# Self attention of a four-layer decoder: queries and keys turned once per entry and fetched per group from a DRAM scratch

## The reference, cut to what matters

```python
for l in range(N_LAYERS):
    h = rmsnorm(x, n1[l])
    q, k, v = jnp.split(h @ Wqkv[l].T + bqkv[l], 3, axis=-1)
    q = apply_rope(split_heads(q, H), cos, sin)      # H = 16, 8 features a head
    k = apply_rope(split_heads(k, H), cos, sin)
    o = merge_heads(sdpa(q, k, v, causal_bias)) @ Wo[l].T + bo[l]
    x = x + o
    ...                                               # cross attention, feed forward
```

## Time and profile before

| | us |
|---|---|
| three runs | 2101.96, 2107.96, 2116.95 |
| median | 2107.96 |
| span of the profiled execution | 2100.9 |
| median less that span | 7.1 |
| self attention of layer 1, first to last tile of maxima | about 1026 to 1210 |

### The profile page before, as it was taken

The page is one execution under the profiler, slowest core; times in us unless marked ns, Lnnn a source line. Parts: engine busy times, 40 slices in busy tenths (PEclk is TensorE's granted clock), DMA queues, the critical chain, the costliest instruction groups (busy, mean ns, idle before and its releaser), DMA issues. The chain is left out here.

```text
span 2100.9 us, 34690 instructions
## 1 busy us (share of the span) xinstructions
PE 1827.5 (87%) x13011; PEld 1120.1 (53%) x13011; DVE 1415.5 (67%) x3427; ACT 1067.7 (51%) x1523; POOL 784.6 (37%) x1131
## 2 busy tenths in 40 slices
PE   5978998594777898899999999999999989989978
PEld 4557664373544444564544565644555554456557
DVE  8667776543676877864577885567786467787475
ACT  2655655131453566564466566366656446656510
POOL 4423324403624453431455342245443155443130
PEclk9999999597787898998999999999999999999989
DMA  7443333121000000141000033000014000003200
GB/s 227 111 137 101 109 104 97 63 69 39 21 1 13 1 1 13 37 110 43 16 1 1 1 93 84 28 1 1 1 44 120 14 16 2 1 26 99 52 1 21
DMA packets 69995, 100.91 MB, mean 48 GB/s; under 512 B 17126, under 2 KB 35438, under 8 KB 69188
## 3 DMA queue, kind: packets, MB, share of 16 engines
q1 hardware_dynamic: 60612, 90.01, 14.9%
q0 software_dynamic: 9216, 8.69, 1.6%
HBM read 52.43 MB, written 12.38 MB: 31 GB/s over the span
## 5 line engine op out<-in xcount | busy, mean ns | idle before, releaser
L1806 DVE TENSOR_REDUCE maxima<-wide 128x2 f32<-128x512 f32 (+3 forms) x512 | 406.1, 819 | 134.2 <-PE wide L836 130.7
L2042 ACT ACTIVATE prob<-wide 128x768 f32<-128x768 f32 (+1 forms) x384 | 332.2, 881 | 149.7 <-PE wide L836 149.4
L1965 ACT ACTIVATE prob<-wide 77x1024 f32<-77x1024 f32 x256 | 257.8, 1017 | 89.8 <-PE wide L836 86.5
L836 PE MATMUL wide<-q_g 32*128 32x256 f32 (+3 forms) x2048 | 268.5, 394 | 37.5 <-ACT prob L2042 18.1
L2284 POOL TENSOR_SCALAR_AFFINE_SELECT prob<-prob 128x256 f32<-128x256 f32 (+1 forms) x384 | 184.9, 487 | 296.4 <-ACT prob L2042 294.6
L1482 DVE TENSOR_REDUCE maxima<-wide 128x8 f32<-128x616 f32 x256 | 202.9, 795 | 110.7 <-PE wide L836 106.7
L836 PEld LDWEIGHTS wide<-q_g 32*128 32x128 f32 x2048 | 140.0, 188 | 205.6 <-issue 100.1
L2106 POOL TENSOR_TENSOR rstd<-moments,cst 128x4 f32<-128x4 f32 x88 | 90.4, 1027 | 360.7 <-DVE moments L1370 173.8
L1886 ACT ACTIVATE q_g<-wide 128x1024 fp32r<-128x1024 f32 x128 | 131.1, 1024 | 179.3 <-PE wide L836 177.4
L1886 ACT ACTIVATE q_g<-acc 128x512 fp32r<-128x512 f32 x192 | 114.5, 596 | 144.0 <-PE acc L836 139.0
L2191 POOL DMA_DIRECT2D masked_k<-kx x224 | 121.2, 546 | 177.4 <-PE wide L836 176.3
(11 more groups left out here) (253 smaller groups left out, 3096.1 us busy)
## 6 DMA issues: line engine op xcount, KB each, us to landing
masked_q<-q_g SPq DMA_DIRECT2D x448, 64.0 KB
masked_q<-mask_l SPq DMA_DIRECT2D x84, 308.0 KB
masked_k<-kx POOLq DMA_DIRECT2D x224, 19.5 KB, 1.9
A<-in_w SPq DMA_DIRECT2D x2, 2048.0 KB, 12.2
unit_w<-in_unit_w SPq DMA_DIRECT2D x8, 448.0 KB, 3.9
ffn_w<-in_ffn_w SPq DMA_DIRECT2D x4, 768.0 KB, 4.7
slots_in<-v_third SPq DMA_DIRECT2D x1, 2560.0 KB, 12.6
prob<-slots_in SPq DMA_DIRECT2D x8, 320.0 KB, 3.1
```

What stands on the lines that cost most here:

```text
L836: return e.matmul(out, lhsT, rhs, start=start, stop=stop, is_transpose=turn)
L1806: e.tensor_reduce(top[:, t, h], v[:, :, at0:at0 + P * t + P], AX.X, ALU.max, negate=True).then_inc(*made("max", *([("free", tile)] if t == ...
L1965: e.activation(p[0:SC, :], s[0:SC, :], ACT.Exp, bias=0.0, scale=1.0).then_inc(*made("exp", pb, ("free", tile)))
L2042: e.activation(pv, sv, ACT.Exp, bias=0.0, scale=8 ** -0.5).then_inc(*made("exp", pb, ("free", tile)))
```

## The change

Queries and keys of an entry are rotated as before (with columns reordered so that a partition after the turn is a feature of a head in a group, and the tables widened to 32 columns and loaded by a DMA of their own, `rope`). `qk_turn` now runs once per entry: eight turns of 128 x 128, one ACT copy back into `qkv`. `qk_cut` takes the high part in one DVE instruction of 128 x 1024 and the low part in one POOL subtraction of 128 x 1024. `qk_store` writes them with three DMAs of 512 KB each into a DRAM scratch (ring of three, 2 MB each) in the row order of the heads; `qk_fetch` brings 128 x 1024 (512 KB) per group into `q_g`. Rows with ones lie in the scratch from three start-up DMAs. After the maxima, DVE writes 32 columns into a small tile, `self_full` is one turn of those 32 columns, ACT copies 32 x 128, and `self_max` lays eight rows of 512 into `q_g` by an SP DMA. In the order, `spread` (turn, cut, store) sits in the prepare of g = 3 at rows 1, 4 and 9, the fetch at row 4 of prepare (13 for the first), and the attend and finish rows are shifted: two logits tiles in attend (rows 8, 10), four in finish (rows 0, 2, 4, 6), where there were four and two. `o_turn` and `out_turn` move to a fifth phase.

```diff
@@ self_steps
+    def spread(b, *rows):
+        return in_rows(*zip(rows, (("qk_turn", l, b), ("qk_cut", l, b), ("qk_store", l, b))))
     def prepare(b, g):
         if (l, b, g) == (0, 0, 0):
-            return in_rows((11, ("qk_turn", l, b, g)))
+            return in_rows((13, ("qk_fetch", l, b, g)))
...
-        phase, c = in_rows((8, ("qk_turn", l, b, g))), b + 1
-        if b and g == 0:
-            phase = beside(in_rows((2, ("cut_k", l, b))), phase)
         if c < B:
             phase = beside(phase, *[[normalise(c)],
                                     [project_in(c), rotate(c, (0, 10))],
-                                    [rotate(c, (1, 1), (2, 3), (3, 6), (4, 8))],
-                                    [rotate(c, (5, 1)), in_rows((4, ("cut_q", l, c)))]][g])
+                                    [rotate(c, (1, 1), (2, 3), (3, 6), (4, 8), (5, 11))],
+                                    [spread(c, 1, 4, 9)]][g])
...
     def attend(b, g):
-        return in_rows((1, ("self_full", l, b, g)), (4, logits(0, 2)), (6, logits(0, 0)), (8, logits(1, 2)),
-                       (10, logits(1, 0)), (12, ("self_values", l, b, g, 0)))
+        return in_rows((1, ("self_full", l, b, g)), (2, ("self_max", l, b, g)), (8, logits(0, 2)), (10, logits(0, 0)))
     def finish(b, g):
-        s = [(0, logits(2)), (2, logits(0)), (4, values(1)), (8, values(2)), (10, values(3))]
+        s = [(0, logits(1, 2)), (2, logits(1, 0)), (4, values(0)), (4, logits(2, 2)), (6, logits(2, 0)), (8, values(1)),
+             (12, values(2)), (12, values(3))]
...
-    turned = beside(rotate(0, *[(k, k // 2) for k in range(6)]), in_rows((3, ("cut_q", l, 0)), (3, ("cut_k", l, 0))),
+    turned = beside(rotate(0, *[(k, k // 2) for k in range(6)]), spread(0, 3, 3, 4),
@@ sync
+            for dram in qk_rows:
+                e.dma_start(dram[:, :].rearrange("(i r x) c -> i r x c", i=HG, x=4)[:, :, 3, :],
+                            io["qk_rows"].unsqueeze(0).broadcast_to([HG, PART, G * 2 * S]))
+            def qk_store(l, b):
+                to = qk_rows[at][:, :].rearrange("(m x) c -> m x c", x=4)
+                for w in need(("sq_top", l, b), ("sq_cut", l, b), T.freed("qk_rows", held)):
+                    e.wait_ge(*w)
+                e.dma_start(to[:, 0, :], t[:, 1:3, :])
+                e.dma_start(to[:, 1, :], t[:, 1::2, :])
+                e.dma_start(to[:, 2, :], t[:, 0::2, :])
+            def qk_fetch(l, b, g):
+                for w in need(("qk_stored", l, b), ("qk_rows",), T.freed("q_g", held)):
+                    e.wait_ge(*w)
+                e.dma_start(q_g[at], of[:, 2 * S * g:2 * S * g + 2 * S])
+            def self_max(l, b, g):
+                for w in need(("mx_turned", l, b, g)):
+                    e.wait_ge(*w)
+                e.dma_start(qk[SELF_MAX:P:SELF_STEP, 0, :].bitcast(F32), mx_t[at].bitcast(F32))
@@ tensor
+                for k in range(2):
+                    for t in range(NI):
+                        i_mm = mm(s[:, S * k + P * t:S * k + P * t + P], src[:, t, k, :], ident, turn=True)
...
-                turn_queries(a, cut_queries(("sqt", l, b)), g)
+                mm(a[0:2 * HG * NI, 0:P], maxima_in[g % 2][:, :, :, :].rearrange("p i k t -> p (i k t)"), ident, turn=True)
```

More of the change, by code:

```diff
@@ L293, in quantised @@
                  [("qkv", 0, b, 0)], [("qkv", 0, b, 1), ("bias_o", 0)]]
-        return [head, tail, [[("rotate", 0, b, k)] for k in range(6)] + [[("cut_q", 0, b)], [("cut_k", 0, b)]]]
+        return [head, tail, [[("rotate", 0, b, k)] for k in range(6)] + [[("qk_turn", 0, b)], [("qk_cut", 0, b)], [],
+                                                                        [("qk_store", 0, b)]]]
     if n == 3:
@@ L561, in build @@
         slots_in, slots_out = (nc.dram_tensor(name, (SLOTS + SPARE, D), F32) for name in ("slots_in", "slots_out"))
-        maxima = [sb(f"maxima{n}", [P, NI, HG]) for n in range(2)]
+        qk_rows = bufs("qk_rows", 3, lambda n: nc.dram_tensor(f"qk_rows{n}", (P, G * 2 * S), F32))
+        maxima = [sb(f"maxima{n}", [P, HG, NI]) for n in range(2)]
+        maxima_in = [sb(f"maxima_in{n}", [P, HG, 2, NI]) for n in range(2)]
         def ps(name, shape):
@@ L669, in heads_of, with parts @@
             return v.rearrange("p (c y r) -> p c y r", y=3, r=VW)[:, :, 0:3:2, :]
-        rot = rope_b[:, :].rearrange("p (t h r) -> p t h r", t=NI, r=8)
+        rot = rope_b[:, :].rearrange("p (t c x) -> p t c x", t=NI, x=HR)
+        cos_sin = cst[:, P:3 * P].rearrange("p (k t x) -> p k t x", k=2, t=NI)
+        raw_qk = qkv[:, :, 0:2 * D]
+        def parts(key):
+            return hid[T.slot("hid", key)]
         def sync(e):
@@ L1126, in bias_o, with qk_turn @@
                     *made("project", ("bias_o", l)))
-            def qk_turn(l, b, g):
-                tile = ("sqk_turn", l, b, g)
-                s = wide[T.slot("wide", tile)]
+            def qk_turn(l, b):
+                tile = ("sqk_turn", l, b)
+                s, src = wide[T.slot("wide", tile)], rope_b[:, :].rearrange("p (t k c) -> p t k c", t=NI, k=2)
                 for w in need(T.freed("wide", tile)):
@@ L1771, in qkv_project @@
                 bias = wt[:, L_BQKV:L_BQKV + 3 * D].unsqueeze(1).broadcast_to([P, 2, 3 * D])
-                for w in need(own(), ("qkv", l, b, half), ("rotated", l, b - 1) if b else None):
+                for w in need(own(), ("qkv", l, b, half), ("sq_cut", l, b - 1) if b else None):
                     e.wait_ge(*w)
@@ L1809, in causal_max @@
                 if k == len(CAUSAL_TILES) - 1:
-                    fill_maxima(cut_queries(("sqt", l, b)), g).then_inc(*made("max_in", ("smax_in", l, b, g)))
+                    into = maxima_in[g % 2]
+                    for w in need(own()):
+                        e.wait_ge(*w)
+                    high_part(into[:, :, 0, :], top[:, :, :]).then_inc(*made("max_in"))
+                    for w in need(own()):
+                        e.wait_ge(*w)
+                    e.tensor_tensor(into[:, :, 1, :], top[:, :, :], into[:, :, 0, :], ALU.subtract).then_inc(
+                        *made("max_in", ("smax_in", l, b, g)))
             def f3_hidden(l, b, c):
@@ L2017, in f1_hidden, with qk_turn, self_full @@
                     *made("silu", ("f1_silu", x8, c, h)))
-            def qk_turn(l, b, g):
-                tile, held = ("sqk_turn", l, b, g), ("sq", l, b, g)
-                s = wide[T.slot("wide", tile)]
-                for w in need(tile, T.freed("q_g", held)):
-                    e.wait_ge(*w)
-                copy(q_g[T.slot("q_g", held)][:, :, :].rearrange("p g s -> p (g s)"), s[:, :]).then_inc(
-                    *made("q", ("sqk_copied", l, b, g), ("free", tile)))
-            def self_full(l, b, g):
-                tile = ("sq_full", l, b, g)
+            def qk_turn(l, b):
+                tile = ("sqk_turn", l, b)
                 for w in need(tile):
                     e.wait_ge(*w)
-                copy(q_g[T.slot("q_g", ("sq", l, b, g))][:, 0, :], acc[T.slot("acc", tile)][:, :]).then_inc(
-                    *made("q", ("sq_filled", l, b, g), ("free", tile)))
+                copy(raw_qk, wide[T.slot("wide", tile)][:, :].rearrange("p (k c) -> p k c", c=2 * D)).then_inc(
+                    *made("q", ("sq_raw", l, b), ("free", tile)))
+            def self_full(l, b, g):
+                tile, held = ("sq_full", l, b, g), ("mx_t", l, b, g)
+                for w in need(tile, T.freed("mx_t", held)):
+                    e.wait_ge(*w)
+                copy(mx_t[T.slot("mx_t", held)], acc[T.slot("acc", tile)][0:2 * HG * NI, 0:P]).then_inc(
+                    *made("q", ("mx_turned", l, b, g), ("free", tile)))
             def self_logits(l, b, g, j, h0):
@@ L2215, in clear @@
                     e.wait_ge(*w)
-                e.memset(k_tok[:, :, :, MROW:MROW + 2], 1.0).then_inc(*made("clear"))
                 for buf in v_self:
```

170 lines of the change are left out of this document (93 added, 77 removed).

## The result

The changed kernel takes 2189.35 us (median of four runs, 2169.95 to 2208.18) against 2105.51 for the kernel before on the same chip: a ratio of 1.0366, 95% interval 1.0307 to 1.0425. The change makes the kernel slower, by 84 us between the medians and by 77 (65 to 89) by the ratio. The forecast was 28 us faster, with a range up to 2130 us; the result lies outside it.

What follows compares the result with a forecast made beforehand. The prediction took PE, busy 87% of the span, as the bound. It summed -77 + 19 + 22 + 6 + 2 = -28 us, so 2108 - 28 = 2080 us, likeliest range 2062 to 2095, 8 in 10 within 2040 to 2130.

Steps and rivals of the forecast that it cites:

- the clock at the starts: Layer starts: a longer wait may bring forward or lengthen PE's half clock; taken as 0, within -3 to +5 a layer.
- The term of -77 us: Self-attention groups: fewer turns on PE save 1.20 us a group over 64 groups, 77 us.
- Rival A: Groups: the gain turns into waits on DVE's last maxima and their transfer; no change, about 2105 us, chance 0.20.
- The start of a layer, 19 us: Each layer's first tile: serial turn, copy, cut, store and fetch cost 4.7 us a layer, 19 us over four.
- The hand-off of the maxima, 22 us: PE's logits in each group: waits on DVE and the maxima transfer cost 0.35 us a group, 22 us.
- B: Rival at the logits: every group waits 1.2 us for the maxima transfer; slower, 2140 us, chance 0.18.
- C: Rival on the DMA queue: group 2's maxima transfer lands 1.5 us late behind an entry's stores; 2098 us, chance 0.08.
- PE's wait at an entry's turn, 6 us: At qk_turn: PE waits 0.5 us for POOL's last rotation, for 12 entries, 6 us.
- The fill, 2 us: Kernel start: 1.5 MB of ones and 128 KB of tables added to the loads, 0 to 6 us, taken as 2.
- The shift of rows: Order of rows: moving two logits tiles from attend to finish conserves work; 0, within 2 us a layer.
- a half clock that spreads over the starts: Layer starts: a sign that the forecast is wrong; no size was given.
- the 9.6 to 9.9 us a group: Middle of a layer: sign for the forecast, a group takes 9.6 to 9.9 us instead of 10.7.

Runs made afterwards that it cites:

- b1: Kernel before with nine of twelve turns a group removed, ACT's copies repeating the turned block; 2105.8 us, ratio 1.001.
- e1: Changed kernel with six idle matmuls of 512 columns (results unused) ahead of PE's wait for the maxima in every group; 2171.9 us, ratio 1.030.
- e2: Changed kernel with nine fp32 turns of the identity (results unused) ahead of PE's wait for the maxima in every group; 2177.8 us, ratio 1.034.
- b3: Kernel before with ACT's copy of each layer's first turned group done six times, so PE stands longer there; 2133.2 us, ratio 1.014.
- b5: Kernel before with nine of twelve turns a group removed and ACT's first copy of each layer done six times; 2125.9 us, ratio 1.013.
- e3: Changed kernel without the transfer that lays the maxima into the turned group; 2193.1 us, ratio 1.043.
- e6: Changed kernel with logits, values and a group's output back in the rows of the kernel before; 2176.0 us, ratio 1.032.
- e8: Changed kernel with the old rows for logits and values, late fill, three idle matmuls a group and twelve at layer starts; 2154.0 us, ratio 1.027.
- e10: Changed kernel with late fill, three idle matmuls a group, twelve at layer starts, entry's turn, cut and store three rows later, projection two later; 2123.2 us, ratio 1.013.
- e7: Changed kernel with the scratch fill late, three idle matmuls a group and twelve at each layer's first tile; 2147.9 us, ratio 1.017.
- e4: Changed kernel with twenty idle matmuls at each layer's first tile of scores; 2204.4 us, ratio 1.047.
- e5: Changed kernel with the scratch's fill of ones issued after the third block's values, not among the first loads; 2193.0 us, ratio 1.042.
- e9: Changed kernel with an entry's turn, cut and store three rows later; 2190.0 us, ratio 1.041.
- e11: Changed kernel with three idle matmuls a group and twelve at layer starts, the scratch fill among the first loads; 2147.5 us, ratio 1.023.
- b2: Kernel before with nine of twelve turns a group removed and three idle matmuls at each group's maxima; 2089.8 us, ratio 0.995.
- b4: Kernel before with three idle matmuls at each group's maxima and nothing else; 2113.5 us, ratio 1.007.

## Why the prediction was wrong

**The step that failed first: the clock at the starts, "0 within -3 to +5 a layer".** There was some 250 us more at half clock (370 in the profiled runs, of which 242 lie in the groups of layers 1 to 3). I looked at the clock only where a longer wait stood, at a layer's start, and not where the work went. The turns that I subtracted as cost also helped to keep PE's clock at the upper level: b1 takes only them away and has 389 us at half clock for 270; e1 and e2 put work back and get 522 down to 343 and 384.

**The term of -77 us.** Its size at the upper clock was wrong too. Of 1.20 us a group b1 shows 0.3 to 0.6 as gained in the groups of the middle: PE's busy time falls by 0.8 to 0.9, and a part of that becomes waiting. I had let DVE's 7.8 us busy a group stand as the next bound and taken all between 10.7 and it as free, although a chain of hand-offs (tile of scores, maxima, tile free again) can bind with every engine idle a part of the time. Rival A said that the gain would turn into waits, though it named the last maxima and their transfer. What grew are PE's waits until DVE frees a tile of scores (58.3 to 108.1 us before weight loads, 20.6 to 29.7 before matmuls), for which the sum had no term. With the clock the gain was nothing in b1, in place of 77.

**The start of a layer, 19 us.** Right in its length, by two misses that cancel: 15.9 us from rotation to first tile, where I had worked out about 16. The stores were issued 5.5 us after the rotation in place of 6.2 (my own terms, with four gaps of 0.15, add up to 6.6), and took 6.6 us until the fetch in place of 5.6; the fetch landed 3.8 us after its issue, for 4.0. b3 prices such a wait at 31 us in the kernel before (21 of waiting, 10 that go with the clock), b5 at 27 where turns are missing.

**The hand-off of the maxima, 22 us, and rivals B and C.** No wait on the transfer shows in the trace, and without it (e3) the time is no shorter. Of the 0.35 us a group that I gave it and DVE together its share was 0; row 8 covers it, and B and C fall. B's mechanism exists where that row is 4: 0.8 to 0.9 us a wait in e6 and e8, close to B's turning point, but 34 and 51 times for 64 groups. B's 2140 lies nearest to the result, for a reason that isn't there.

**PE's wait at an entry's turn, 6 us.** Measured 13.1 us in ten waits, 1.3 each in place of 0.5. A second one of the same kind, on ACT's normalised rows, I had missed: PE, with less to do, reaches every row earlier than the chains of the next entry. e10 shows that they are worth some 9 to 24 us, once the clock is held.

**The fill, 2 us.** 10.1 us in the first 60 us, and of the order of 10 still at the first tile of layer 0.

**The shift of rows, "conserves work: 0, within 2 us a layer".** A loss of 9 to 13 us in all with the low clock (e6, not clear of the noise), and a gain of 6 to 21 with the clock held (e8 against e7): it is what hides the transfer.

The sum as the runs show it: turns 0 (b1), starts 27 to 31 (b3, b5), the fill some 10, together about 40 of the 77 to 84 us. The other 40 have no price of their own. Idle matmuls with a late fill take 42 away (e7) and the later rows 9 more, 51 in all (e10), which is about the fill and these 40, and leaves about the price of the starts; e4, e5 and e9 alone took nothing. So the rest goes away when the clock is held and PE's waits in the groups are shortened; how it divides between the two isn't settled. The last of the signs that I had named as speaking against the forecast was the right one: a half clock that spreads over the starts. Of the signs for it, the first tile at 16 us, the wait on q_g once a layer and the turns from 12 to 3 came true, and the 9.6 to 9.9 us a group did not (8.9 to 11.6 in the four groups at the upper clock shown above).

## What to carry to other kernels

Before subtracting work from an engine whose granted clock has moved in the trace, ask what the clock row of the stretch will be without that work: here taking nine turns a group away gained 0.3 to 0.6 us in each group at the upper level and cost the same again in clock. PE busy at over 90% was no proof that all of its work was the bound: up to two thirds of what it no longer did turned into waits for hand-offs. Taking work off an engine also moves every fixed row of the order closer to the chains that feed it, so move those rows in the same edit. Price an edit with the clock held as well as without: the old order of rows gained 9 to 13 us at a mean clock of 0.89 (e6) and lost 6 to 21 at 0.91 and more (e8). The turn's move (e9, and in e10 with the projection's) and the fill (e5, and e7 with e11) point the same way, less cleanly.

## What the runs showed of the hardware that was not expected

The clock can be bought: three matmuls of 512 columns a group, about 0.2 us each, took 12 us off a kernel that lacked nine turns a group (b2 against b1) and cost 15 us in one that had them (b4).

Nine turns in fp32 a group kept the clock up nearly as well as six bf16 matmuls of 512 columns (0.914 and 0.919).

A single turn to 32 columns is not the quarter of four that I had put it at. In the changed kernel, layer 2, by form (busy us, mean ns):

```profile
L884 PE MATMUL acc<-cst,maxima_in 128*32 128x128 f32 x10 | 3.5, 351 | 3.1 <-DVE maxima_in L1860 3.1
```

At the upper level one is busy for 0.27 us in the traces, and the next matmul starts 0.20 us after it where nothing is waited for (0.15 in my sum), 0.35 at the lower level.
